# A decoder layer with transposed QKV products, scattered score operands and scores on two 64-row tiles

## The reference

```python
x = x + attn(layernorm(x))            # causal, 32 query heads, 8 key/value heads, head size 16, rope
x = x + cross(layernorm(x), ctx)      # one head of 512, ctx is 2 x 512 tokens, no mask
x = x + ffn(layernorm(x))             # down(gate(h) * up(h)), inner size 1376, weights made ternary
# attn: q, k = rope(h @ Wq), rope(h @ Wk); softmax(mask(q k^T / 4)) (h @ Wv) @ Wo, 4 query heads share a key head
# ffn weights: s = mean|w|; w' = round(clip(w / (s + 1e-5), -1, 1)) * s
```

## Time and profile before

| | |
|---|---|
| median of three runs | 250.87 us |
| span of the profiled execution | 247.7 us |
| PE busy / its share | 236.1 us, 95% |
| DVE, ACT, POOL busy | 141.0, 119.0, 35.7 us |
| granted TensorE clock, mean | 0.998 |
| DMA traffic | 19.96 MB |

### The profile page before, as it was taken

One profiled execution on the slowest core, in us unless ns is written; L12 is line 12 of the kernel. 1 busy time (PEld: TensorE's weight loads), 2 busy tenths in 40 slices (PEclk: granted clock), 3 DMA queues, 4 the chain that ended last, 5 costly groups with the idle time before them and its releaser, 6 DMA issues.

```text
span 247.7 us, 4047 instructions
## 1 busy us (share of the span) xinstructions
PE 236.1 (95%) x1494; PEld 162.9 (66%) x1502; DVE 141.0 (57%) x337; ACT 119.0 (48%) x199; POOL 35.7 (14%) x62
## 2 busy tenths in 40 slices
PE   7799998999999999999999989799999999999992
PEld 2367756677767776647776454578888778767770
DVE  2687377866565557459624256977456654353232
ACT  2036577366757636842574672454743223322330
POOL 3330000621132214130210111000000000000000
PEclk9999999999999999999999999999999999999999
DMA  6999100000560180336000053000000000020002
GB/s 179 385 404 404 46 0 1 1 3 8 225 228 1 34 309 3 102 114 246 1 1 0 5 191 148 3 1 1 3 0 0 3 0 0 3 85 0 3 0 86
DMA packets 8980, 19.96 MB, mean 81 GB/s; under 512 B 1056, under 2 KB 1440, under 8 KB 8960
## 3 DMA queue, kind: packets, MB, share of 16 engines
q1 hardware_dynamic: 8384, 19.60, 22.0%
q10 hardware_dynamic: 576, 0.10, 0.2%
HBM read 18.58 MB, written 1.05 MB: 79 GB/s over the span
## 4 chain that ended last, share of the span: by engine, by line
PE 90%; DVE 5%; issue 1%; DMA 1%; ACT 0%; DVEq 0%; POOL 0%; POOLq 0%
PE ps L1191 15%; PE ps L1030 9%; PE ps L1206 7%; PE ps L1056 7%; PE ps L1082 6%; PE ps L1129 6%; PE ps L1038 4%; PE ps L1293 4%; PE ps L1259 4%; PE ps L1017 4%; PE ps L1307 3%; PE ps L1263 3%; PE ps L1144 3%; PE ps L1113 3%; PE ps L1248 2%; PE ps L1087 2%
## 5 line engine op out<-in xcount | busy, mean ns | idle before, releaser
L497 POOL TENSOR_SCALAR_AFFINE_SELECT prob<-prob 128x512 f32<-128x512 f32 x32 | 19.6, 637 | 97.9 <-ACT prob L693 97.9
L693 ACT ACTIVATE prob<-ps 128x1536 f32<-128x1536 f32 x16 | 23.1, 1446 | 10.0 <-PE ps L1296 10.0
L1030 PE MATMUL ps<-wqkv,xnT 128*128 128x512 f32 (+1 forms) x64 | 22.4, 494 | 1.4 <-ACT xnT L514 0.7
L1003 DVE TENSOR_REDUCE mx<-ps 128x4 f32<-128x512 f32 x16 | 11.1, 691 | 18.7 <-PE ps L1263 18.7
L1191 PE MATMUL ps<-h_hi,gate_q 128*128 128x256 f16 (+1 forms) x88 | 20.4, 273 | 0.0
L1191 PE MATMUL ps<-h_lo,up_q 128*128 128x256 f16 (+1 forms) x88 | 20.4, 273 | 0.0
L1191 PE MATMUL ps<-h_lo,gate_q 128*128 128x256 f16 (+1 forms) x88 | 20.4, 273 | 0.0
L1191 PE MATMUL ps<-h_hi,up_q 128*128 128x256 f16 (+1 forms) x88 | 20.4, 272 | 0.0
L581 ACT CAST in_hi<-inter 128x256 f16<-128x256 f32 (+1 forms) x22 | 8.9, 405 | 23.4 <-DVE inter L879 23.4
L1005 DVE TENSOR_REDUCE mx<-ps 128x4 f32<-128x1024 f32 x16 | 19.4, 1213 | 0.0
L879 DVE TENSOR_TENSOR inter<-gate_s,ps 128x256 f32<-128x256 f32 (+1 forms) x22 | 9.2, 419 | 16.4 <-PE ps L1191 14.9
(11 more groups left out here) (166 smaller groups left out, 482.2 us busy)
## 6 DMA issues: line engine op xcount, KB each, us to landing
raw<-gate_dram SPq DMA_DIRECT2D x1, 2752.0 KB, 17.2
raw<-up_dram SPq DMA_DIRECT2D x4, 688.0 KB, 4.7
ctxT<-ctxT_dram SPq DMA_DIRECT2D x2, 1024.0 KB, 5.4
ctx_n<-ctx_dram SPq DMA_DIRECT2D x2, 1024.0 KB, 7.7
wqkv<-wqkv_dram SPq DMA_DIRECT2D x4, 384.0 KB, 6.4
raw<-down_dram SPq DMA_DIRECT2D x2, 768.0 KB, 4.5
x<-x_dram SPq DMA_DIRECT2D x4, 256.0 KB, 5.8
xwq<-xwq_dram SPq DMA_DIRECT2D x1, 1024.0 KB, 9.2
```

What stands on the lines that cost most here:

```text
L497: nc.gpsimd.affine_select(out=v, in_=v, compare_op=ALU.is_ge, fill=0.0, base=0, pattern=[[0, GROUP], [1, P]], channel_multiplier=-1).then_ ...
L693: nc.scalar.activation(prob[:, i % 2, :], ps[:, 3:6, :].rearrange("p a b -> p (a b)"), ACT.Exp, scale=DH ** -0.5).then_inc(exp_done, 1)
L1003: nc.vector.tensor_reduce(mx[:, i % 2, 0, :], bank(0).rearrange("p (h k) -> p h k", h=GROUP), AX.X, ALU.max).then_inc(max_done, 1)
L1030: mm = nc.tensor.matmul(out, xnT[:, k, t * P:(t + 1) * P], wqkv[:, k, lo:hi], start=(k == 0), stop=(k == KD - 1))
```

## The change

- The projection is transposed: weights are the stationary operand, all 512 tokens stream. Both sides are split into high and low first (weights: high on ACT, low on POOL, 24 pieces each; x: ACT and DVE), and high x high, high x low, low x high are multiplied in f32r. Keys and values come first (in two halves of 256 tokens), then two "pairs" of query products. The rope is a product with tables whose partitions are lanes (`tables_T`); the values are transposed back (`values_T`).
- Rotated and split keys and queries go to their places in `ks` and `qs` by DMA instead of by PE: 36 copies of 128 KB on SP's queue, each from 128 partitions to 16 partitions that are 8 apart. `ks`, `qs` are zeroed before (DVE, ACT, POOL). The projection of all tiles is finished before the loop; "pq", "pk", "rot", "hi", "lo", "st" are gone from the table, and two "a" pieces come ahead of the loop (`BEFORE`).
- Two of a group's heads lie in rows 0 to 63, two in rows 64 to 127, and the score products alternate between the two.
- Tiles 2 and 3 are normalised by ACT; statistics of the next tile come before the normalisation of the last.
- In the loop, PE does `scores_by_query(it)` first and `maxima_T(it)` last in the same step; DVE copies `mT(it)` at the end of the step behind all side pieces, and ACT does slot 0 ahead of the exponential. The rest of `BESIDE` is spread anew.
- The gate weights are loaded from ACT's queue, behind the last projection, since their place is used by the weights before.

```diff
+        BEFORE = [("a", 0, 0), ("a", 0, 1)]
...
-            ([("abs", 0, 1)], [], [("pq", 3), ("abs", 0, 2)]),
-            ([("rot", 3, 0)], [("st", 10), ("abs", 0, 3)], [("part", 0), ("pk", 3), ("hi", 3, 0)]),
-            ([("rot", 3, 1)], [("hi", 3, 1), ("lo", 3, 0)], [("a", 0, 0), ("whole", 0, 0)]),
-            ([("lo", 3, 1), ("st", 11)], [("st", 12)],
-             [("a", 0, 1), ("whole", 0, 1), ("tern", 0, 0), ("whole", 0, 2)]),
...
+            ([("a", 1, 0)], [], [("u", 0)]),
+            ([("a", 1, 1)], [], [("u", 1)]),
+            ([("abs", 0, 0)], [("abs", 0, 1)], [("a", 2, 0)]),
+            ([("abs", 0, 2)], [("abs", 0, 3)], [("c",)]),
+            ([("part", 0)], [], [("a", 2, 1)]),
+            ([("whole", 0, 0), ("whole", 0, 1)], [("tern", 0, 0)], [("tern", 0, 1), ("whole", 0, 2), ("whole", 0, 3)]),
+            ([("tern", 0, 2)], [("tern", 0, 3)], [("a", 3, 0)]),
+            ([], [], [("a", 3, 1)]),
+            ([], [], []),
+            ([("abs", 1, 0)], [("abs", 1, 1)], []),
+            ([("abs", 1, 2)], [("abs", 1, 3)], []),
+            ([("part", 1)], [("cc", 0)], []),
+            ([("cc", 1), ("whole", 1, 0), ("whole", 1, 1)], [("tern", 1, 0)],
+             [("wo", 0), ("whole", 1, 2), ("whole", 1, 3), ("tern", 1, 1)]),
+            ([("wo", 1), ("tern", 1, 2)], [("tern", 1, 3)], [("n2", 0)]),
+            ([("xT", 1, 0), ("n2", 1)], [("xT", 1, 1)], [("high", "wo", 0)]),
+            ([("g", 0, 0), ("low", "wo", 0), ("high", "wo", 1)], [],
+             [("g", 0, 1), ("low", "wo", 1), ("high", "wo", 2), ("low", "wo", 2), ("high", "wo", 3), ("low", "wo", 3)]),
+            ([("xs", 0), ("abs", 2, 0)], [("abs", 2, 1)], [("xs", 1), ("abs", 2, 2)]),
+            ([("xpT", 0), ("abs", 2, 3)], [("abs", 2, 4)], [("xpT", 1), ("xo", 0)]),
+            ([("part", 2), ("n3", 0), ("xo", 1)], [], [("xT", 2, 0)]),
+            ([("n3", 1), ("hl", 0), ("whole", 2, 0), ("tern", 2, 0)], [("cc", 2)],
+             [("xT", 2, 1), ("hl", 1), ("whole", 2, 1), ("whole", 2, 2), ("tern", 2, 1), ("whole", 2, 3),
+              ("whole", 2, 4), ("tern", 2, 2)]),
...
+            def scatter_k(b):
+                for high, copies in ((True, (0, 2)), (False, (1,))):
+                    sp.wait_ge(hi_ready if high else lo_ready, 2 if high else 1)
+                    if not high:
+                        sp.wait_ge(k_low_copied, 1)
+                    for c in copies:
+                        for o in range(2):
+                            src = (roped_hi if high else roped_lo)[:, 0, o, b * T:(b + 1) * T]
+                            sp.dma_start(ks[2 * c + o:P:8, b, :, :].bitcast(F32), src.bitcast(F32)
+                                         ).then_inc(k_placed[b], 16)
+
+            def scatter_q(pair, b, o):
+                if o == 0 and pair == 1:
+                    sp.wait_ge(q_zeroed[b], 1)
+                for high, copies in ((True, (0, 1)), (False, (2,))):
+                    sp.wait_ge(hi_ready if high else lo_ready, 2 * pair + o + (1 if high else 0))
+                    src = (roped_hi if high else roped_lo)[:, pair % 2, o, b * T:(b + 1) * T]
+                    for c in copies:
+                        sp.dma_start(qs[2 * c + o:P:8, b, 8 * (pair - 1):8 * pair, :].bitcast(F32), src.bitcast(F32)
+                                     ).then_inc(q_placed[b][pair - 1], 16)
+
+            scatter_k(0)
+            for o in range(2):
+                scatter_q(1, 0, o)
+            scatter_k(1)
+
+            LATER_SCATTER = [(2, 0, 0), (2, 0, 1), (1, 1, 0), (1, 1, 1), (2, 1, 0), (2, 1, 1)]
...
+            def high_roped(pair, o):
+
+                act.wait_ge(roped_ready, 2 * pair + o + 1)
+                if pair == 2:
+                    for b in range(B):
+                        act.wait_ge(k_placed[b], 16 * 6)
+                nc.scalar.copy(roped_hi[:, pair % 2, o, :], turned[:, pair % 2, o, :]).then_inc(hi_ready, 1)
...
+            def low_roped(pair):
+
+                s = pair % 2
+                for o in range(2):
+                    dve.wait_ge(hi_ready, 2 * pair + o + 1)
+                    if pair == 2 and o == 0:
+                        for b in range(B):
+                            dve.wait_ge(k_placed[b], 16 * 6)
+                    nc.vector.tensor_tensor(roped_lo[:, s, o, :], turned[:, s, o, :],
+                                            roped_hi[:, s, o, :].bitcast(F32), ALU.subtract).then_inc(lo_ready, 1)
...
+            raw_k = raw[:, 0:KD * INNER].rearrange("p (k n) -> p k n", k=KD)
+            for k in range(KD):
+                act.dma_start(raw_k[:, k, :], gate_d[k * P:(k + 1) * P, :]).then_inc(raw_in, 16)
+            side(BEFORE[0:1])
+            high_roped(2, 0)
+            side(BEFORE[1:2])
...
+                side(beside(it, 0))
...
-                side(beside(it, 0) + beside(it, 1))
+                side(beside(it, 1))
...
+                side(beside(it, 0))
                 side(beside(it, 1) + beside(it, 2))
+                if it in COLUMN_AT:
+                    take_column(COLUMN_AT[it])
+                i = it
+                if i < NG:
+                    dve.wait_ge(mT_ps, i + 1)
+                    if i >= 2:
+                        dve.wait_ge(m_placed[i % 2], 32 * (i // 2))
+                    nc.vector.tensor_scalar(mT[:, i % 2, :], ps[0:2 * GROUP, 0, 0:P], -1.0, None, ALU.mult
+                                            ).then_inc(m_sb, 1)
...
+            def high_weights(kind, k):
+
+                if kind == 0:
+                    act.wait_ge(wqkv_in[k], 16)
+                for to, w in zip(packed(kind, wqkv_hi[:, k, :]), loaded(kind, wqkv[:, k, :])):
+                    ins = nc.scalar.copy(to, w)
+                ins.then_inc(w_high, 1)
...
+            start(0)
+            start(1)
+            normalise(0, lambda: None)
+            start(2)
+            normalise(1, lambda: None)
+            start(3)
+            for t in range(TT):
+                low_tile(t)
+            rotate(0)
+            low_keys()
+            rotate(1)
+            low_roped(1)
...
+            def project(pair):
+
+                if pair == 2:
+                    pe.wait_ge(rope_read, 2)
+                    pe.wait_ge(vT_sb, 1)
+                for o in range(2):
+                    out = bank(PAIR_BANK[pair] + o)
+                    cols = slice((2 * pair + o) * P, (2 * pair + o + 1) * P)
+                    for k in range(KD):
+                        pe.wait_ge(w_high, KD * pair + k + 1)
+                        for right in (xnT_hi, xnT_lo):
+                            nc.tensor.matmul(out, wqkv_hi[:, k, cols], right[:, k, :],
+                                             start=(k == 0 and right is xnT_hi), stop=False)
+                    for k in range(KD):
+                        pe.wait_ge(w_low, KD * pair + k + 1)
+                        mm = nc.tensor.matmul(out, low_weights(k)[:, cols], xnT_hi[:, k, :], start=False,
+                                              stop=(k == KD - 1))
+                    mm.then_inc(qkv_ps, 1)
...
+            keep_busy(4)
+            tile_T(1)
+            keep_busy(4)
+            tile_T(2)
+            keep_busy(2)
+            keys_high(0)
             tile_T(3)
-            stacks(0)
+            keys_low(0)
+            keys_high(1)
+            keys_low(1)
+            tables_T()
+            project(1)
+            values_T()
+            project(2)
             pe.wait_ge(rope_read, 4)
-            pe.wait_ge(v_sb, 2)
-            pe.wait_ge(xnT_sb, 3)
-            project(qkv_bank(2)[:, 0:D], 2, 0).then_inc(qkv_ps, 1)
-            stacks(1)
-            project(qkv_bank(2)[:, D:QKV], 2, 1).then_inc(qkv_ps, 1)
+            side_products(BEFORE)
...
+                mask_late(1)
+                early(0, 0)
+                late(1, 0)
+                early(0, 1).then_inc(first_rows, 1)
+                late(1, 1)
+                if i >= 1:
+                    pe.wait_ge(m_sb, i)
+                mask_late(0)
+                late(0, 0)
+                late(0, 1)
+                pe.wait_ge(first_rows, i + 1)
+                early(1, 0)
...
+                early(0)
+                late(1).then_inc(second_rows, 1)
+                early(1)
+                pe.wait_ge(second_rows, i + 1)
+                late(0).then_inc(sT_ps, 1)
...
-                    column_sum(COLUMN_AT[it])
-                if 0 <= it - 1 < NG:
-                    maxima_T(it - 1)
+                if it < NG:
+                    scores_by_query(it)
+                side_products(beside(it, 0))
                 if 0 <= it - 2 < NG:
                     scores_by_key(it - 2)
-                side_products(beside(it, 0))
-                if it < NG:
-                    scores_by_query(it)
                 side_products(beside(it, 1))
                 if 0 <= it - 3 < NG:
                     weighted_values(it - 3)
                 side_products(beside(it, 2))
+                if it in COLUMN_AT:
```

(7 more changed lines are left out.)

643 lines of the change are left out of this document (314 added, 329 removed), and 5 rows, old and new, of the table BESIDE.

## The result

The changed kernel takes 288.92 us (median of four executions, 285.01 to 291.01) against 250.14 in the same job: 1.150 times the time before, 95% interval 1.141 to 1.159. The forecast was 258.0, range 247 to 265. The four executions come with mean granted clocks of 0.910, 0.893, 0.887 and 0.881 in the order of their times; the profiled one is the last, span 289.2 us. Each ratio in this document leaves out the executions that lie more than 1.5% above the fastest of their kernel, here the one of 291.01 us.

A forecast was written before the change was run, and what follows sets the result against it. PE was taken as the bound, until something else ends last. Start 5.2, steps 0 to 11 -2.6, steps 12 to 15 -0.1, end 5.0 gave +7.5 on 250.87: 258.4, written as 258, range 247 to 265.

The forecast's parts named there:

- What bounds the kernel: Steps 0 to 15: PE is the bound, others have air; the change makes PE 13.6 us lighter.
- The clock: Rival: clock falls to 1.2 GHz at 8 to 15 us and in step 5, giving 264; chance 0.06.
- The start: Before the loop: first scores at 35.5 us instead of 30.3, +5.2 us.
- ACT's gate load shares the DMA engines: At the start: named beside DVE's chain, with no size of its own.
- Step 0: 7.2 us: rounding of the second query pair waits for all 12 key copies, put at 38.
- Steps 5 to 7: 18.7 us: in step 5 "tern" waits for POOL's chunk ahead of oT; PE has nothing for 4 us.
- Steps 8 to 11: 19.1 us: no "a" fills them; 3.85 a step without side work, 5.2 with passes around the exponential.
- Steps 12 to 15: 34.3 us instead of 34.4: mT behind DVE's side pieces loses 2.8 and 1.3, the second xT 1.4.
- The end of the loop: Step 16 to wo(2): 29.8 us instead of 25.6; with a later cc 3, +5.0 us there and on.
- The two 64-row tiles: Score products: overlap of about 1.6, 1.11 to 0.7 us; masks and scores together 1.3 instead of 1.65.
- From span to time: Whole kernel: median of the runs lies 3.2 above the span, so span 255.2 becomes time 258.4.
- The rival on the other side: Rival: small copies oT (steps 3 to 10) and mT (steps 12, 13) come in time, 13.2 less, 245; chance 0.15.

The follow-up runs named there:

- e11: The kernel before with four additional ACT copies ahead of the copy oT in step 6, making PE wait: 260.55 us against 249.61, ratio 1.041.
- e4: Changed kernel with score products reordered so that rows 0 to 63 and rows 64 to 127 no longer alternate: 289.75 us, one execution.
- e7: Changed kernel with the first "tern" piece behind oT in step 5 and POOL rounding its chunks ahead of the causal cut: 276.58 us.
- e2: Changed kernel with additional PE products nobody reads, before the loop and in later steps, no wait removed: 277.85 us.
- e1: Changed kernel with ACT issuing the four gate loads behind the rounding of the last query pair: 285.06 us.
- e6: Changed kernel with the last query pair's high and low part made in step 0 of the loop, the gate load behind them: 283.17 us.
- e8: Changed kernel with the edits of e6, e3 and e7, and the last weight's "tern" pieces later at the loop's end: 254.86 us, ratio 1.017.
- e5: Changed kernel with e2's unread PE products (7 instead of 38 before the loop) and e1's late gate load: 267.71 us.
- e3: Changed kernel with ACT's loop passes behind the copy oT and DVE copying mT ahead of its slot 2 pieces: 268.37 us.
- e10: e8 plus a third side product before the loop, gate load in halves, some passes and xT later, four unread PE products: 249.46 us, ratio 0.995.

## Why the prediction was wrong, point by point

**What bounds the kernel.** "PE work that is taken away pays, until something else ends last" was right, and left out that PE's speed depends on its being kept at work. The kernel before let it wait for 0.7 us at most in steps 0 to 15; losing that cost more (27 us by the estimate above) than the 13.6 us of products gave.

**The clock** is the step that failed. I had it as a rival with 0.06 and priced it by "3 us of work" at each of two places. The runs show six stretches at the lower level, 3.4 to 20.5 us long and 68.3 in all, that begin in or just behind waits of 1.7 us and more; for one wait of 5.00 us the lower level lasts 10.2 us and costs 4.7 (e11). Of the two places, the one from 8 to 15 us kept its clock in this profile; e4 to e7 have 3.4 us at the lower level there. I had read the right sign in the trace (no idle stretch above 2 us, hence no row for the price) and from the missing row took a small price instead of an open one. With the 13 us of span that e2 gave back in place of the 6, the rival's time would have been 271; with the estimate of 27 us, 286.

**The start**, 45.4 for 35.5. PE's own part was right: first tile transposed at 7.94 (7.9), side products done at 35.8 (34.8). "ACT's gate load shares the DMA engines" was named and given no price; it was 8.1 us (e1). The other 1.9 are in e1 still: 1.0 in PE's own part, and its wait for the copies, 1.58 us.

**Step 0**, 9.3 for 7.2: mechanism right (e6 and e8 bring it to 7.4 and 5.9), part of the excess is the low clock.

**Steps 5 to 7**: `oT` behind "tern" behind POOL's chunk, shown by e7; 5.41 us, not 4.0, and 8.8 us of work at the lower level, half of which, 4.4, is an estimate of a cost that wasn't in the sum. **Steps 8 to 11**: with the clock held up 20.6 (e5), for 19.1; without passes around the exponential 17.9 (e3). **Steps 12 to 15**: the wait for `m_sb` was 2.71 at the start of step 13 (2.8 forecast). The second, 1.3, didn't come; in its place `oT` in step 14 waited 2.14 behind "tern". With the filling the stretch took 38.3 (e2) and 40.0 (e5), with one and two low stretches of 3.4 us inside; with 1.7 off for each (an estimate) both come to 36.6, so 34.3 was some 2 too low.

**The end of the loop**: 29.6 for 29.8, the chain as worked out, and 2.0 of it is "tern" (2,0) ahead of `cc` 2 (e8). **The two 64-row tiles**: scores 1.29 us (1.3), by a worse overlap and fewer gaps than taken.

**From span to time**: the 3.2 us that I added set the span of one execution against the median of three. Within one execution the two differ by 1.7 to 2.1 us (291.01 and 289.2 here), so the forecast should have been 257.

**The rival on the other side**, small copies in time, was priced 13.2. e3 took most of these waits away and gained 20.5: right place, and half again as much, for the clock. With the gate load late and the clock mostly held (e5), 12 us of the excess are left: 5.7 in steps 12 to 15, of which filling and two low stretches are a part, 2.3 at the start, the rest in steps 0 and 5 to 11.

## What to carry to other kernels

A wait of PE can cost nearly twice its length, since the clock comes back late: 9.7 us for 5.00 (e11). So when a tuned kernel keeps PE at 95%, a change that takes work from PE and lets it wait even once must be priced with the clock, and where no wait exists in the trace to read the price from, it is an unknown with a wide range. Large loads that nobody needs soon belong behind the small copies that open the next stage, on whichever queue they are issued, and copies that PE waits for belong ahead of passes that nobody waits for.

## What I had not expected of the hardware

Behind a wait of 5 us the lower clock lasts 7.9 to 10.0 us under work that leaves hardly a gap (e11: 10.00 of 10.00 us busy at a mean clock of 0.54; the changed kernel behind its waits of 9.65 and 5.41: 7.9 us with 7.5 busy, and 9.0 with 9.0). The length of the wait doesn't say the length of the fall: behind 1.71 us came 20.5 (steps 10 to 12), behind 2.71 only 3.4, behind 2.14 13.7, all in the changed kernel. In the profiled execution of e10 it fell at the end of step 8 with no wait over 0.5 us in steps 6 to 8, PE being busy 4.11 to 4.52 of each 5 us there; other executions of the same program are at 0.998 and 1.00. The Trainium skill (TensorE: Matmul & The Clock Gate, A second HAM failure mode) tells of such falls from short gaps between groups; these executions agree, which of the gaps does it they don't show. The fall in step 13 of e5, behind 10 us in which PE is busy all the time, neither this nor a wait explains.
